# Four-head attention over 2500 nodes: the third head's scores move, in every second unit, from VectorE to ScalarE and GpSimd

## The reference, cut to what matters

```python
h = (x_flat @ W_gat).reshape(M, HEADS, NUM_EXPERTS)          # 2500 x 4 heads x 4
a_src = (h * att_src).sum(-1); a_dst = (h * att_dst).sum(-1)
e = leaky_relu(a_src[src] + a_dst[dst], negative_slope=0.2)
e_max = segment_max(e, dst); ee = exp(e - e_max[dst])
denom = segment_sum(ee, dst)
alpha = ee / (denom[dst] + 1e-16)
agg = segment_sum(h[src] * alpha[:, :, None], dst)
```

## Time and profile before

| what | value |
|---|---|
| median of 3 executions | 6163.33 us (6162.44 to 6171.94) |
| the profiled execution's own time | 6217.01 us |
| its span in the profile | 6215.2 us |
| mean granted TensorE clock | 0.877 of full |
| busy: TensorE matmul, VectorE, ScalarE, GpSimd | 80%, 56%, 26%, 51% of the span |
| the stage of the change, first score to last prob | 4237.6 to 4689.7 us of the span |

### The profile page before, as it was taken

How to read it: one execution, slowest core, us unless ns; L and a number is a source line. 1 busy time by engine, 2 the same in 40 slices (tenths; PEclk the granted TensorE clock), 3 DMA queues, 4 the chain that set the end, 5 groups by cost and what they waited for, 6 DMA issues and landing times.

```text
span 6215.2 us, 70248 instructions
## 1 busy us (share of the span) xinstructions
PE 4982.6 (80%) x23435; PEld 2962.0 (48%) x23497; DVE 3507.5 (56%) x7225; ACT 1630.9 (26%) x2765; POOL 3156.6 (51%) x2151
## 2 busy tenths in 40 slices
PE   5777767766999889988578794376765998999999
PEld 3444444444555665576566563373222333222266
DVE  6766555653566211111344310399996999777754
ACT  2111111112222002200231210126773001666521
POOL 5768888888888777877677768302220000000000
PEclk8887777676999889998787797699998999999999
DMA  7767666666544875587998776894443010323200
GB/s 185 153 138 136 122 127 122 127 96 57 11 16 8 97 67 19 12 93 70 171 128 79 52 83 24 113 206 110 110 112 80 29 29 23 82 80 82 78 15 27
DMA packets 558579, 523.31 MB, mean 84 GB/s; under 512 B 263641, under 2 KB 489874, under 8 KB 557159
## 3 DMA queue, kind: packets, MB, share of 16 engines
q1 hardware_dynamic: 295560, 427.90, 31.9%
q0 software_dynamic: 261696, 90.13, 25.1%
q10 hardware_dynamic: 1028, 1.52, 0.1%
HBM read 365.58 MB, written 153.75 MB: 84 GB/s over the span
## 4 chain that ended last, share of the span: by engine, by line
POOL 27%; PE 23%; DMA 20%; issue 15%; DVE 10%; SPq 5%; ACT 1%; DVEq 0%; POOLq 0%; ACTq 0%
POOL pairs L724 22%; DMA pairs<-PAIR_CNT,PAIR_IDX 13%; PE PS L2346 6%; PE PS L2183 5%; SPq L187 4%; DVE WORK L1987 4%; DVE MXS L2224 4%; DMA WORK<-x_table,WORK 4%; POOL sums L776 3%; DMA sums<-WORK,XT 3%; POOL WORK L763 2%; PE PS L1011 2%; PE PS L983 2%; PE PS L2204 2%; PE PS L601 2%
## 5 line engine op out<-in xcount | busy, mean ns | idle before, releaser
L724 POOL DMA_INDIRECT pairs<-PAIR_CNT,PAIR_IDX x1364 | 2151.3, 1577 | 608.8 <-issue 433.5
L776 POOL DMA_INDIRECT sums<-WORK,XT x340 | 531.0, 1562 | 180.3 <-issue 101.8
L601 PE MATMUL PS<-WORK,IDENT 125*125 125x256 f32 x680 | 305.9, 542 | 359.4 <-DMA WORK<-x_table,WORK 358.8
L515 DVE SCALAR_TENSOR_TENSOR XT<-PS,ROWS 128x512 f32<-128x512 f32 x704 | 483.0, 746 | 144.0 <-PE PS L501 143.5
L2417 DVE SCALAR_TENSOR_TENSOR WORK<-WORK 125x1000 f32<-125x1000 f32 x400 | 462.2, 1197 | 152.8 <-ACT WORK L2385 152.1
L1627 PE MATMUL PS<-IDENT,WORK 125*125 125x125 f32 x1920 | 259.4, 304 | 279.4 <-DMA WORK<-pairs 194.9
L1661 DVE CUSTOM_DVE_ANT_0 ROWS<-ROWS 125x1250 f32<-125x1250 f32 x200 | 280.8, 1457 | 346.2 <-ACT ROWS L1647 346.2
L2183 PE MATMUL PS<-ROWS 32*125 32x500 f32 x3200 | 451.3, 633 | 28.8 <-DVE MXS L2224 19.2
L2224 DVE TENSOR_REDUCE MXS<-PS 125x4 f32<-125x2000 f32 x200 | 438.8, 2235 | 22.5 <-PE PS L2204 18.5
L2385 ACT ACTIVATE WORK<-PS 125x1000 f32<-125x1000 f32 x400 | 380.0, 1002 | 239.5 <-PE PS L2334 239.5
L644 ACT ACTIVATE WORK<-PS 125x256 f32<-125x256 f32 x340 | 131.0, 385 | 1158.8 <-PE PS L601 1158.8
(11 more groups left out here) (338 smaller groups left out, 8100.3 us busy)
## 6 DMA issues: line engine op xcount, KB each, us to landing
WORK<-pairs SPq DMA_DIRECT2D x400, 218.8 KB
pairs<-ROWS SPq DMA_DIRECT2D x75, 976.6 KB, 7.2
WORK<-pairs SPq DMA_DIRECT2D x48, 1093.8 KB
WORK<-pairs SPq DMA_DIRECT2D x80, 546.9 KB
pairs<-PAIR_CNT,PAIR_IDX POOLq DMA_INDIRECT x1364, 4.1
WORK<-pairs SPq DMA_DIRECT2D x40, 382.8 KB
XT<-pairs SPq DMA_DIRECT2D x12, 1093.8 KB
mask_t<-ROWS SPq DMA_DIRECT2D x40, 273.4 KB
```

The lines of the kernel that those rows point to most:

```text
L515: dve.scalar_tensor_tensor(junk[0:lanes, q, 0:SUPER * lanes], PS[0:lanes, bank, 0:SUPER * lanes], cols[0:lanes, at], weights, ALU.is_equal ...
L601: pe.matmul(PS[0:P, 2 + k % 2, 0:D], IDENT[0:P, 0:P], GATH[0:P, k % 8, :], start=False, stop=True).then_inc(sem("edge_added"), 1)
L724: pool.indirect_dma_start(table, bass.IndirectOffsetOnAxis(idx[:, n:n + 1], 0), cnt[:, n:n + 1], None, compute_op=ALU.add).then_inc(sem(do ...
L776: pool.indirect_dma_start(sums[c], bass.IndirectOffsetOnAxis(SROW[:, k:k + 1], 0), SUMMED[:, k % 8, :], None, compute_op=ALU.add).then_inc ...
```

## The change

In even units n, `rectified(n)` is (2, 3): the third head (h = 2), too, is rectified by ScalarE and added by GpSimd, and VectorE makes two scores only. Odd units stay as they are. The row that ScalarE rectifies for the third head, 0.8 d, is a ninth row per chunk: its source column is `C20[3]` (one more instruction in the stage ahead) and its place is the memory of the four PAIR tiles, which become one tile `PAIR` with four views of the same sizes and order. `ROW_LAG` goes from 3 to 2. The waits count the scores and additions of the new order.

```diff
-        PAIR_IDX = sb("PAIR_IDX", [P2, K2], I32)
-        PAIR_CNT = sb("PAIR_CNT", [P2, K2])
-        PAIR1_IDX = sb("PAIR1_IDX", [128, K1], I32)
-        PAIR1_CNT = sb("PAIR1_CNT", [128, K1])
+        PAIR = sb("PAIR", [128, 2 * K2 + 2 * K1])
+        PAIR_IDX, PAIR_CNT = PAIR[:, 0:K2].bitcast(I32), PAIR[:, K2:2 * K2]
+        PAIR1_IDX, PAIR1_CNT = PAIR[:, 2 * K2:2 * K2 + K1].bitcast(I32), PAIR[:, 2 * K2 + K1:2 * K2 + 2 * K1]
...
                 st.go(dve.tensor_scalar(r1[:, :, 3:4], dst[:, :, 3:4], 0.8, None, ALU.mult))
+                st.go(dve.tensor_scalar(C20[3][:].unsqueeze(2), dst[:, :, 2:3], 0.8, None, ALU.mult))
...
-        J_ROWS, ROW_LAG = 8, 3
+        J_ROWS, ROW_LAG = 9, 2
+        ROW_THIRD = PAIR[0:P, 0:N]
+
+        def attention_rows():
+            return shift_rows(4) + [(C20[3][:], ROW_THIRD)]
+
+        def rectified(n):
+            return (3,) if n % 2 else (2, 3)
+
+        def rectified_before(n):
+            return n + (n + 1) // 2
...
-                act.activation(J_E[n % 3][:, 3, :], ROWS[0:P, 3, c * CH:(c + 1) * CH], ACT.Relu,
-                               bias=GAT[2][:, t, 3:4]).then_inc(sem("l2j_rect"), 1)
+                for h in rectified(n):
+                    row = ROWS[0:P, 3, :] if h == 3 else ROW_THIRD
+                    act.activation(J_E[n % 3][:, h, :], row[:, c * CH:(c + 1) * CH], ACT.Relu,
+                                   bias=GAT[2][:, t, h:h + 1]).then_inc(sem("l2j_rect"), 1)
...
-                    if h == 3:
-                        act.wait_ge(sem("l2j_fourth"), n + 1)
+                    if h in rectified(n):
+                        act.wait_ge(sem("l2j_fourth"), rectified_before(n) + rectified(n).index(h) + 1)
                     else:
-                        act.wait_ge(sem("l2j_score"), 3 * n + h + 1)
+                        act.wait_ge(sem("l2j_score"), 4 * n - rectified_before(n) + h + 1)
...
-                pool.wait_ge(sem("l2j_rect"), n + 1)
-                pool.tensor_tensor(J_E[n % 3][:, 3, :], J_E[n % 3][:, 3, :], ROWS[0:P, 7, c * CH:(c + 1) * CH], ALU.add
-                                   ).then_inc(sem("l2j_fourth"), 1)
+                for i, h in enumerate(rectified(n)):
+                    pool.wait_ge(sem("l2j_rect"), rectified_before(n) + i + 1)
+                    pool.tensor_tensor(J_E[n % 3][:, h, :], J_E[n % 3][:, h, :], ROWS[0:P, 4 + h, c * CH:(c + 1) * CH],
+                                       ALU.add).then_inc(sem("l2j_fourth"), 1)
...
-                for h in range(3):
+                for h in range(4 - len(rectified(n))):
                     dve.scalar_tensor_tensor(J_E[n % 3][:, h, :], ROWS[0:P, h, cols], GAT[2][:, t, h:h + 1],
                                              ROWS[0:P, 4 + h, cols], ALU.add, ALU.max).then_inc(sem("l2j_score"), 1)
```

More of the change, by code:

```diff
@@ L1903, in row @@
                     pe.wait_ge(sem("l2j_row"), r - 2)
-                spread_row(pe, shift_rows(4), row_of(r), ROW_BANK + r % 3).then_inc(sem("l2j_spread"), 1)
+                spread_row(pe, attention_rows(), row_of(r), ROW_BANK + r % 3).then_inc(sem("l2j_spread"), 1)
             for r in range(J_ROWS):
@@ L1938, in rectify @@
                 act.wait_ge(sem("l2j_row"), J_ROWS * (c + 1))
-                act.activation(J_E[n % 3][:, 3, :], ROWS[0:P, 3, c * CH:(c + 1) * CH], ACT.Relu,
-                               bias=GAT[2][:, t, 3:4]).then_inc(sem("l2j_rect"), 1)
+                for h in rectified(n):
+                    row = ROWS[0:P, 3, :] if h == 3 else ROW_THIRD
+                    act.activation(J_E[n % 3][:, h, :], row[:, c * CH:(c + 1) * CH], ACT.Relu,
+                                   bias=GAT[2][:, t, h:h + 1]).then_inc(sem("l2j_rect"), 1)
             def row(r):
                 act.wait_ge(sem("l2j_spread"), r + 1)
-                keep_row(act, shift_rows(4), row_of(r), ROW_BANK + r % 3).then_inc(sem("l2j_row"), 1)
+                keep_row(act, attention_rows(), row_of(r), ROW_BANK + r % 3).then_inc(sem("l2j_row"), 1)
             for r in range(J_ROWS):
```

## The result

The changed kernel takes 6209.41 us (median of 4 executions, 6196.76 to 6217.62) against 6165.20 for the kernel before (4 executions, 6162.44 to 6171.94): ratio 1.0076, 95% interval 1.0054 to 1.0097. The forecast was 6211. The change moved 50 scores away from the engine that bounds the stage, and the kernel became 44 us slower.

The account below looks back on a forecast made before the run. VectorE alone was taken to bound the stage. Pairs of units going from 9.02 to 9.97 us gave +47.0 and the ninth row +0.9, so +48 on the median 6163.3: 6211 us, range 6188 to 6234.

Parts of the forecast that it names:

- VectorE alone bounds the stage: In the stage of scores and probs VectorE is busy 90.00 of 90.00 us; the stage takes 452.1 us for 100 units.
- Even unit, +1.00: GpSimd's second addition comes between VectorE's two scores and delays the second: +1.00 us per even unit.
- Odd unit, +0.60: GpSimd's addition starts only 0.05 ahead of the first score, which loses 1.01 instead of 0.41: +0.60 us.
- ScalarE doesn't bind: With 50 more rectifications ScalarE needs about 7.5 us of a pair's 9.97, so it doesn't bind in the main case.
- The ninth row, +0.9: In chunk 0 ScalarE copies one more row ahead of the first score: +0.9 us; the four later ones are hidden.
- rival 4: TensorE's clock falls to 1.2 GHz in longer units, costing 4 per pair; ten pairs give 6251 us; chance 0.05.
- The sum on the median: +47.0 and +0.9 make +48 us, put on the median 6163.3, not on the profiled execution's 6217.0: 6211 us.
- Rival 1: Even units: the second addition finds no gap between the scores and runs beside prob at no cost: 6162 us, chance 0.12.
- Rivals 2 and 3: Second: collisions stay as now, 6132 us, chance 0.07; third: GpSimd keeps its turn over both additions, 6224 us, chance 0.08.

Follow-up runs that it names:

- the early version: The changed kernel with ScalarE rectifying the next unit's heads ahead of its four exponentials: 6147.85 us against 6203.09 for the kernel before, ratio 0.9902.
- The third experiment: The changed kernel with only the rectification for odd units taken ahead of the exponentials: stage 452.0 us, time 6214.8 in its one execution.
- the memsets: The changed kernel with GpSimd's 150 additions replaced by memsets of the same buffers, which only write SBUF: stage 383.6 us.

## Why the prediction was right

The stage was forecast at about 499 us and came at 499.5, the time at 6211 and came at 6209.4. Point by point:

- *VectorE alone bounds the stage.* Holds: it is busy 310.00 of 310.00 in the window above, and stays so even in the early version, but for the waits around the 20th unit.
- *Even unit, +1.00.* Predicted 4.86 between probs, measured 4.85 to 4.86. It rested on an inference, that the second addition gets its turn between two scores, with no row of two queued additions. The rows now show it, and show that GpSimd's next addition starts 0.04 before the last one's end. I had bounded the gap by 0 and 0.31, so it lay just outside; the second addition's record is 1.68 and not 1.56 for that reason, and its end is where it was predicted, since it waits for the score in any case.
- *Odd unit, +0.60.* Predicted 5.11, measured 5.12, with the addition 0.04 ahead of the score (0.05 predicted). The third experiment isolates it.
- *ScalarE doesn't bind.* Holds in the changed kernel; at 265.65 of 285 in the early version it is near.
- *The ninth row, +0.9.* Its own price is 0.87. The opening grew by 1.3 in the profile; the other 0.4 are the first rows, which came slower while the granted clock was 0.53 (4167.5 to 4172.0), and lie inside what the opening differs by between profiles.
- *Missed:* rival 4 saw that TensorE would be spread thinner, and put 0 on it in the main case. The clock does fall, in stretches mostly of 3.4 us, to 1.2 GHz, but VectorE doesn't notice in this kernel: the probs keep their spacing. The prediction also has no term for what lies behind the stage, and there the span's rest is 3.9 to 4.2 longer, 3.8 of it within 131 us of the last prob. The first half-clock stretch behind the stage lasts 51.2 us in both profiles of the changed kernel and 44.4 before, but its length doesn't decide it: with one addition left out it is 47.8 and the rest 1530.2, in the kernel before with the earlier rectification it is 47.8 too and the rest 1526.1. What makes the 3.9 stays open.
- *The sum on the median.* 47.3 for the stage, 1.3 ahead, 3.9 behind give 52.5 in the profiles; the medians differ by 44.2, with an interval of 33 to 60 (1.0054 and 1.0097 of 6165). The close hit of 2 us is luck: the stage's 47 us is what the prediction earned, the 3.9 behind had no term, and the scatter ahead of the stage is larger than either. Run beside the experiments, the kernel before took 6201 to 6207 us, not 6165.
- *Rival 1*, the Trainium skill's "for the whole instruction" read over overlapping scores ("SBUF — State Buffer", "Who interferes with whom"), is refuted by every even unit: the addition comes between scores whose records overlap by 0.07. The same section's statement that a GpSimd instruction that only writes does not contend agrees with the memsets. *Rivals 2 and 3* left no score of theirs: no odd unit's first score of 1.14, no score of 2.4.

## What to carry to other kernels

Where GpSimd works beside VectorE, count not its instructions but where they fall: beside a VectorE instruction with one SBUF input and one from PSUM an addition cost nothing, beside one with two SBUF inputs it cost about what was left of it less 0.2, up to 1.0 us for 500 columns (1.75 instead of 0.73). Moving work off a saturated engine can slow it when the receiver excludes it; try first to shift the helper's start, here one number in ScalarE's order, which shortened the stage by 37 us in the old kernel (452.1 to 414.9) and by 102 in the new one (499.5 to 397.9). With it the new kernel is 1.0% faster than the old one; the same number alone makes the old one 0.6% faster. When a stage gets shorter, look at what was loaded with just enough lead; here one 2.4 MB load showed up as a wait of 4.8 us.

## What the runs showed of the hardware that was not expected

- The waiting engine gets its turn between back-to-back instructions of the other, so contention interleaves one by one: addition, score, addition, score, in every even unit. Both scores are held there, the first for 1.14 and the second for 1.72 instead of 0.73.
- The turn is handed over at a constant distance: a held score ended 0.53 to 0.54 after the addition and a held addition 1.10 to 1.12 after the score, in all nine profiles with additions. Whether the handover itself costs something in these distances isn't shown.
- TensorE's granted clock went from 1.00 to 0.94 in 4300 to 4610, with idle stretches ahead of values of 1.94 us as a rule and 2.2 at most, instead of 1.6. Its busy share fell only from 72% (224 of 310) to 71% (220 of 310), but that hides work that took twice as long: at 1.00 the same work in units of 4.99 instead of 4.51 would have been about 65%, an estimate from these rows. In the kernels whose units are all shorter than before the clock was 1.00 in 4320 to 4600; with only the odd units short and the even ones at 4.85 it was 0.94.
- A half-clock stretch of TensorE can reach VectorE two units later by way of a buffer: values late, rectification late, addition further into a score (nine times in the third experiment, 0.3 us each).
